# Twelve decoder stages on one Trainium2 core: other numbers of identity products at 18 calls and in the attention ramps, query rows issued from ScalarE, LayerNorm tails of two feed-forwards reordered

## The reference, cut to what matters

```
x = LN(x + L0_attn(x));   x = LN(x + L0_xattn(ctx, x)); x = LN(x + L0_ffn(x))
x = LN(x + L1_attn(x));   x = LN(x + L1_xattn(x, ctx)); x = LN(x + L1_ffn(x))
x = LN(x + L2_attn(x));   x = LN(x + L2_xattn(x, ctx)); x = LN(x + L2_ffn(x))
x = LN(x + L3_attn(x));   x = LN(x + L3_xattn(ctx, x)); x = LN(x + L3_ffn(x))
```

## Time and profile before

| | |
|---|---|
| median of 3 runs | 2351.48 us (2344.88 to 2352.47) |
| the profiled execution | 2345.65 us |
| its span, first to last instruction | 2343.8 us |
| TensorE busy (share of the span) | 2112.0 us (90%), 25065 products |
| VectorE, ScalarE, GpSimd busy | 1330.4, 1129.5, 967.9 us |
| identity products of `stay_busy`, L583 | 575 |

### The profile page before, as it was taken

How to read it: one execution, slowest core, us unless ns; L and a number is a source line. 1 busy time by engine, 2 the same in 40 slices (tenths; PEclk the granted TensorE clock), 3 DMA queues, 4 the chain that set the end, 5 groups by cost and what they waited for, 6 DMA issues and landing times. The chain is left out here.

```text
span 2343.8 us, 60484 instructions
## 1 busy us (share of the span) xinstructions
PE 2112.0 (90%) x25065; PEld 1276.9 (54%) x25109; DVE 1330.4 (57%) x3369; ACT 1129.5 (48%) x2592; POOL 967.9 (41%) x865
## 2 busy tenths in 40 slices
PE   5998999889987899999999999999879989899894
PEld 3445666645543555555555555555544557455563
DVE  3535454447835776777777776767436533467233
ACT  1333455115532676766667776767514402235321
POOL 2010000020125887878888787878310023200023
PEclk9999999999998999999999999999989989989897
DMA  2110000000002021211121111211000024000321
GB/s 68 26 36 1 2 1 1 1 15 6 3 1 75 18 61 28 48 41 43 36 52 33 49 33 37 60 27 43 18 8 13 2 61 143 16 13 2 103 69 44
DMA packets 70577, 78.54 MB, mean 34 GB/s; under 512 B 10624, under 2 KB 48649, under 8 KB 70306
## 3 DMA queue, kind: packets, MB, share of 16 engines
q1 hardware_dynamic: 64114, 61.75, 10.1%
q0 software_dynamic: 3696, 10.56, 1.5%
q10 hardware_dynamic: 2496, 2.36, 0.5%
HBM read 40.90 MB, written 6.82 MB: 20 GB/s over the span
## 5 line engine op out<-in xcount | busy, mean ns | idle before, releaser
L3573 POOL TENSOR_TENSOR l1fb_rinv<-l1fb_ssq,neghalf 128x8 f32<-128x8 f32 x192 | 316.0, 1646 | 160.6 <-DVE l1fb_ssq L3616 158.1
L3716 ACT ACTIVATE l1fb_p<-ps,l1fb_shift 128x64 f32<-128x64 f32 x768 | 177.7, 315 | 159.0 <-PE ps L3873 137.7
L3575 POOL TENSOR_TENSOR l1fb_qk<-l1fb_qk,l1fb_r 128x512 f32<-128x512 f32 x192 | 244.1, 1271 | 0.0
L3780 PE MATMUL ps<-l1fb_wqkv,l1fb_xs 128*128 128x512 f32 x384 | 219.2, 654 | 6.3 <-DVE l1fb_r L3626 6.2
L3577 POOL TENSOR_TENSOR l1fb_qk<-l1fb_qk,l1fb_rinv 128x512 f32<-128x512 f32 x192 | 200.2, 1042 | 15.1
L3626 DVE TENSOR_TENSOR l1fb_r<-ps,l1fb_turn_tab 128x256 f32<-128x256 f32 x384 | 142.8, 413 | 0.0
L3623 DVE TENSOR_TENSOR l1fb_qk<-ps,l1fb_turn_tab 128x512 f32<-128x512 f32 x192 | 132.2, 689 | 14.4 <-POOL l1fb_qk L3575 12.5
L583 PE MATMUL ps<-ident_b 128*128 128x512 bf16 x575 | 133.8, 389 | 3.5 <-PEq L671 1.7
L3614 DVE TENSOR_REDUCE l1fb_ssq<-l1fb_sq 128x8 f32<-128x512 f32 x192 | 129.7, 675 | 2.7 <-ACT l1fb_sq L3696 2.7
L3696 ACT ACTIVATE l1fb_sq<-ps 128x512 f32<-128x512 f32 x192 | 118.7, 618 | 11.7 <-PE ps L3780 10.9
L3724 ACT ACTIVATE l1fb_both<-ps 128x512 f32<-128x512 f32 (+1 forms) x194 | 117.3, 604 | 8.3 <-PE ps L3873 7.8
(11 more groups left out here) (728 smaller groups left out, 4817.9 us busy)
## 6 DMA issues: line engine op xcount, KB each, us to landing
l1fb_v<-l1fb_v SPq DMA_DIRECT2D x48, 260.0 KB, 4.3
l1fb_v<-l1fb_v SPq DMA_DIRECT2D x48, 195.0 KB, 3.9
l1fb_wqkv<-in_L_ffn_Wqkv SPq DMA_DIRECT2D x24, 256.0 KB, 2.9
l3f_w<-in_L_ffn_W SPq DMA_DIRECT2D x21, 256.0 KB, 6.8
l1fb_wqkv<-in_L_ffn_Wqkv SPq DMA_DIRECT2D x6, 512.0 KB, 5.1
l1fb_wo<-in_L_ffn_Wo SPq DMA_DIRECT2D x6, 512.0 KB, 4.1
l1fb_w<-in_L_ffn_W SPq DMA_DIRECT2D x6, 341.0 KB, 3.0
l3f_xs<-zeros SPq DMA_DIRECT2D x1, 1344.0 KB, 7.1
```

The source lines that it names most:

```text
L3573: nc.gpsimd.tensor_tensor(w.rinv[:, u, :], w.ssq[:, u, :], chip.neghalf[:, 0:8], ALU.pow).then_inc(*w.unit_norm.end(f"rinv{u}"))
L3575: nc.gpsimd.tensor_tensor(w.qk[:, u, :], w.qk[:, u, :], fp(w.r2), ALU.add).then_inc(*w.unit_norm.end(f"add{u}"))
L3716: last = nc.scalar.activation(w.p[:, c % 2, q, j, :], ps[:, SCORE_BANK + j, q * SEEN:(q + 1) * SEEN], ACT.Exp, bias=w.shift[:, c, j, q:q + 1])
L3780: nc.tensor.matmul(ps[:, PROJ_BANK(u), :], w.xs[:, x.odd, q * P:(q + 1) * P], w.wqkv[:, col:col + 512], start=True, stop=True)\
```

## The change

Numbers of identity products (`stay_busy`) at 18 calls, before -> after:

| stage | head | end |
|---|---|---|
| l0_attn | 18 -> 26, 24 -> 18 | |
| l0_xattn | 19 -> 23 | 24 -> 28 |
| l0_ffn | | 6 -> 8 |
| l1_attn | 9 -> 13, 37 -> 31 | 7 -> 11 |
| l1_xattn | | 12 -> 16 |
| l1_ffn (enter, leave) | 14 -> 20 | 44 -> 27 |
| l2_attn | 24 -> 18 | 9 -> 14 |
| l2_xattn | | 6 -> 10 |
| l2_ffn | 95 -> 99 | 80 -> 78 |
| l3_attn | | 13 -> 18 |
| l3_xattn | 28 -> 24 | |

In the ramp of the three stages without a mask, each step gets two more in front of the first bank's product. `ahead` becomes a table by slot: l2_attn 8 in front of group 0 as before and now 8 in front of group 2, l1_attn now 5 in front of group 0. The four query DMAs of batch 0 go from SyncE to ScalarE, right behind ScalarE's copy of the queries (in l1_attn behind its copy of `xT1`, since VectorE makes the queries there). The tail of L1_ffn is done for all four batches together with four sets of buffers, and that of L2_ffn batch by batch with each batch's last step put behind the next batch's statistics.

```diff
+def strips_load_begin(eng, h, q1, q_ready):
+    eng.wait_ge(*h.padded_q.of(0))
+    eng.wait_ge(*q_ready)
+    strips_load_queries(eng, h, 0, 0, q1)
...
 def strips_load(eng, h, i, q1, k1, q_ready, k_ready):
...
-        for at in range(0, P, STRIP):
-            eng.dma_start(h.q[at:at + h.hd, :, b, :], q1[at:at + STRIP, i, n * S:(n + 1) * S]).then_inc(*h.heads_in[b].landed())
+        if b:
+            strips_load_queries(eng, h, i, n, q1)
...
-        if (t, u, i, p) == (0, 0, 0, 0):
-            stay_busy(nc, chip, 3 + h.bank(b, g, u, i), ahead)
+        if (u, i, p) == (0, 0, 0) and t in ahead:
+            if n_of(b, g, u, i) >= 3:
+                eng.wait_ge(*h.exped.of(n_of(b, g, u, i) - 3))
+            stay_busy(nc, chip, 3 + h.bank(b, g, u, i), ahead[t])
...
                     scores_free(slot, u, i)
+                    stay_busy(nc, chip, h.bank(*h.group(slot), u, i), 2 - 2 * i)
...
             nc.scalar.activation(q1[:, 0, :], ps[:, 7, :], ACT.Copy, scale=scale).then_inc(*act.end("q0"))
+            strips_load_begin(eng, h, q1, act.done("q0"))
...
@@ l2_ffn @@
-                tails_dve(nc, eng, chip, t[PAIR * pair:], dve, pool, pair, lambda i: gathered[PAIR * pair + i].of(QT - 1),
+            for b in range(B):
+                eng.wait_ge(*gathered[b].of(QT - 1))
+                nc.vector.tensor_tensor(fp(t[b].y), of(back, b), of(kept, b), ALU.add).then_inc(*dve.end(f"sum{b}"))
+                tail_stats(nc, eng, t[b], dve, b)
+                tail_var(nc, eng, chip, t[b], dve, b)
+                if b:
+                    tail_normed(nc, eng, chip, t[b - 1], dve, pool, b - 1)
+            tail_normed(nc, eng, chip, t[B - 1], dve, pool, B - 1)
...
@@ l1_ffn_leave @@
-                nc.vector.tensor_copy(fp(xb), chip.x_tok[:, b, :, :]).then_inc(*dve.end("x"))
-                tail_dve(nc, eng, chip, t, dve, pool, b, chip.ps[:, b, 0:S].rearrange("p (t d) -> p t d", t=QT), fp(xb))
+                eng.wait_ge(*pe.done(f"y{b}"))
+                nc.vector.tensor_tensor(fp(t[b].y), chip.ps[:, b, 0:S].rearrange("p (t d) -> p t d", t=QT), chip.x_tok[:, b, :, :], ALU.add)\
+                    .then_inc(*dve.end(f"sum{b}"))
+            for b in range(B):
+                tail_stats(nc, eng, t[b], dve, b)
+            for b in range(B):
+                tail_var(nc, eng, chip, t[b], dve, b)
+            for b in range(B):
+                tail_normed(nc, eng, chip, t[b], dve, pool, b)
```

More of the change, by code:

```diff
@@ L123, in tail_pool, with tail_stats, tail_var, tail_normed @@
     nc.gpsimd.tensor_tensor(fp(t.rstd), fp(t.rstd), chip.neghalf[:, 0:QT], ALU.pow).then_inc(*pool.end("rstd" + of))
+def tail_stats(nc, eng, t, dve, b):
+    eng.wait_ge(*dve.done(f"sum{b}"))
+    for q in range(QT):
+        last = nc.vector.bn_stats(t.stats[:, q, :], t.y[:, q, :])
+    last.then_inc(*dve.end(f"stats{b}"))
+def tail_var(nc, eng, chip, t, dve, b):
+    eng.wait_ge(*dve.done(f"stats{b}"))
+    nc.vector.memset(chip.scratch[:, 4 + b:5 + b], 0.0)
+    for q in range(QT):
+        last = nc.vector.bn_aggr(t.mv[:, q, :], t.stats[:, q, :])
+    last.then_inc(*dve.end(f"var{b}"))
+def tail_normed(nc, eng, chip, t, dve, pool, b):
+    eng.wait_ge(*pool.done(f"rstd{b}"))
+    for q in range(QT):
+        last = nc.vector.tensor_scalar(chip.x_tok[:, b, q, :], t.y[:, q, :], t.mv[:, q, 0:1], t.rstd[:, q:q + 1], ALU.subtract, ALU.mult)
+    last.then_inc(*dve.end(f"normed{b}"))
+def tail_root(nc, eng, chip, t, dve, pool, b):
+    eng.wait_ge(*dve.done(f"var{b}"))
+    nc.gpsimd.tensor_tensor(fp(t.rstd), t.mv[:, :, 1], chip.eps[:, 0:QT], ALU.add).then_inc(*pool.end(f"vareps{b}"))
+    eng.wait_ge(*pool.done(f"vareps{b}"))
+    nc.gpsimd.tensor_tensor(fp(t.rstd), fp(t.rstd), chip.neghalf[:, 0:QT], ALU.pow).then_inc(*pool.end(f"rstd{b}"))
 def named(names, i):
@@ L316, in strips_pad_keys, with strips_pe @@
     last.then_inc(*h.padded_k.one())
-def strips_pe(nc, eng, chip, h, vhead, v_ready, mask=None, early=None, late=None, ahead=0):
+def strips_pe(nc, eng, chip, h, vhead, v_ready, mask=None, early=None, late=None, ahead={}):
     ps = chip.ps
+    n_of = lambda b, g, u, i: 2 * h.pair(b, g, u) + i
     def scores_free(t, u, i):
@@ L1086, in early @@
                     eng.wait_ge(*dve.done("v1"))
[L1088 to L1089 removed]
+            strips_pe(nc, eng, chip, h, lambda i: i, lambda i: dve.done(f"v{i}"), early=early, ahead={0: 8, 2: 8})
+            stay_busy(nc, chip, 0, 14)
 LAMBDA_INIT = 0.8 - 0.6 * float(np.exp(-0.3 * 12))
@@ L1266, in late @@
                     strips_out(nc, eng, chip, h, b, attT, w["L1_attn_Wo"], None)
-            strips_pe(nc, eng, chip, h, lambda i: i // 2, lambda i: dve.done(f"v{i}"), early=early, late=late)
-            stay_busy(nc, chip, 0, 7)
+            strips_pe(nc, eng, chip, h, lambda i: i // 2, lambda i: dve.done(f"v{i}"), early=early, late=late, ahead={0: 5})
+            stay_busy(nc, chip, 0, 11)
 def paired(names):
@@ L2733, in _ @@
                     .then_inc(*gathered[q // QT].landed())
-            for pair in range(B // PAIR):
-                tails_pool(nc, eng, chip, t[PAIR * pair:], dve, pool, pair)
+            for b in range(B):
+                tail_root(nc, eng, chip, t[b], dve, pool, b)
         @block.vector
@@ L3348, in l1_ffn_leave @@
     with ExitStack() as ctx:
-        sb = lambda n, s, dt=F32: ctx.enter_context(nc.sbuf_tensor(f"l1fl_{n}", s, dt))
         pe_s, dve_s, act_s, pool_s, loads = stage_sems(nc, ctx, "l1fl")
-        t = Tail(nc, ctx, "l1fl")
-        xb = sb("xb", [P, QT, D])
-        pe, dve, pool = Steps(pe_s, ["y"]), Steps(dve_s, ["x"] + TAIL_DVE), Steps(pool_s, TAIL_POOL)
+        t = [Tail(nc, ctx, f"l1fl{b}") for b in range(B)]
+        each = lambda name: [f"{name}{b}" for b in range(B)]
+        pe, dve = Steps(pe_s, each("y")), Steps(dve_s, each("sum") + each("stats") + each("var") + each("normed"))
+        pool = Steps(pool_s, [f"{name}{b}" for b in range(B) for name in TAIL_POOL])
         block = ctx.enter_context(nc.Block())
@@ L3373, in _ @@
                     last = nc.tensor.transpose(chip.ps[:, b, q * P:(q + 1) * P], f.xr[:, b, q * P:(q + 1) * P], chip.ident[:, :])
-                last.then_inc(*pe.end("y"))
-            stay_busy(nc, chip, 5, 44)
+                last.then_inc(*pe.end(f"y{b}"))
+            stay_busy(nc, chip, 5, 27)
 class FfnWork:
```

49 lines of the change are left out of this document (27 added, 22 removed).

## The result

The changed kernel takes 2334.98 us (median of 6 runs, 2326.19 to 2340.53) where the kernel before takes 2351.97 beside it. The ratio is 0.9937, 95% interval [0.9918, 0.9956]. Run twice more on other chips it gave 0.9907 [0.987, 0.9945] and 0.9946 [0.9924, 0.9968]. So it is faster by about 15 us by the ratio (17 by the two medians), where 30.5 against the median had been forecast: the direction was right, the size about half.

What follows compares the result with a forecast made beforehand. TensorE was taken as the bound in nine low-clock stretches, besides its waits for DMAs and barriers. Terms -9.8 + 6.1 + 0 - 4.0 - 0.3 - 18.5 = -26.5 us from 2345.65 gave 2319.2, adjusted to 2321 us; range 2309 to 2340.

Steps and rivals of the forecast that it cites:

- part 1: Four strips stages: batch 0's query DMAs on ScalarE make key DMAs land sooner, -9.8 us (5.7 to 11.4).
- part 5: Nine low-clock stretches: filled waits hold TensorE's clock, three quarters of 25 us regained, -18.5 us (0 to -25).
- Rival (b): l1_attn and l3_xattn: transfers bound the landing, nothing moves there, 4.1 us less gain, 2325 us; chance 0.14.
- The side condition: Strips stages' heads: identity products cut by 4 or 6, 0.9 or 1.3 us, so they end before the new landing.
- Part 2: Ramps of l1_attn, l2_attn, l3_xattn: two more products per step and the `ahead` products cost +6.1 us (3 to 16).
- The forecast of steps: l3_xattn's ramp: all sixteen steps 2.24 us or, behind an `early`, 0.44 longer than before, at clock 1.00.
- Rival (c): Ramps: added products do not hold the high clock and run at the low one, +9.9 us, 2356; chance 0.05.
- Part 3: Heads and ends: twelve calls grow by 2 to 8 products, each covered by a longer wait, cost 0.
- Part 4: Tails: L1_ffn's batches together -4.0 us (-3.5 to -4.4), L2_ffn's last block -0.3 us (0 to -1.3).
- the nine stretches: Low-clock stretches just behind added work, 61.3 us together at 1.2 GHz, TensorE busy 58.7; few should stay at 0.50.
- (a): Whole kernel: the clock does not follow, stretches fall elsewhere, only parts 1, 2 and 4 remain, 2338 us; chance 0.19.
- some 40 us: Whole kernel: the clock's low time must fall by this much, or the prediction is wrong.

Runs made afterwards that it cites:

- The four parts alone: Kernel before with one part each: batch 0's queries on ScalarE, 0.9987; ramps' products, 0.9972; two tails, 0.9977; longer series at heads and ends, 0.9957.
- `e_tails`: Kernel before with the two tails alone (L1_ffn's batches together with 27 products, L2_ffn's batch by batch with 78): ratio 0.9977.
- `a_hl`: Changed kernel with longer identity series at the four heads (25, 36, 22, 49) and products in L1_ffn's layers: 2319.94 us, ratio 0.9875.
- `e_start`: Kernel before with only batch 0's query DMAs moved to ScalarE and four heads cut by 4 or 6 products: ratio 0.9987.

## Why the prediction was right or wrong

**Direction and the two largest terms' signs: right.** The sum of -26.5 us was -8.0 without the clock and -18.5 of clock. Measured are -3.6 +- 0.8 without the clock, and 25 and 41 us less low clock on the two chips, 33 in the mean, which at 0.337 is -11. The four parts alone sum to -1.0 +- 2.1 at equal clock, as they should within the errors, but to 61 us less low clock: that is where they do not add. Two terms are too large, part 1 and part 5, each by some 7 us.

**Part 1, -9.8 us: wrong, the step that failed first.** The keys did leave 2.7 to 3.1 us sooner. What failed is the step from there to the landing. For l0_attn and l2_attn the text took the full 2.85 us ("the issue sets the pace") and the profiles gave 1.5 and 2.2. For l1_attn and l3_xattn it took 1.8 and 2.3 and they gave -1.1 and +0.3. Together that is 2.9 us for 9.8, and alone the part measured -2.3 +- 0.7 in the executions. The reading behind it was of the DMA share: 0.27 and 0.49 looked like room, and "the first transfers had idle engines". In the changed kernel the share stands at such a value from the first packet to the last, in l1_attn already before the change (0.20, 0.28, 0.27, 0.27 in windows of 2 us from 495 to 503). Rival (b), that the transfers bound these two stages, was right and had been given 0.14. It had no term for the loss in l1_attn, where packets take longer on two queues. The rule of the Trainium skill (Trainium Kernel Development and Optimization, Key Constraints), that issuing from several engines saves issue time only, agrees with gains that stay below the 2.85 us of issue time, 1.5, 2.2 and 0.3; it doesn't tell of l1_attn's loss of 1.1 us. The side condition was missed too: the heads' products were cut for a landing that did not come, and left waits of 5.0 and 3.2 us.

**Part 2, +6.1 us: right in kind, a little high**: +4.5 +- 0.8, within its ends of 3 and 16. The forecast of steps held at 2.24 us. Rival (c), ramps at the low clock, did not appear.

**Part 3, 0: right**: -1.5 +- 0.8 at equal clock.

**Part 4, -4.3 us**: the tail is 4.4 us shorter and L1_ffn's end 4.1 us (4.3 in `e_tails`), where -4.0 was taken: right, with the mechanism that the text named, products at the low clock that end at 1737.28 (forecast 1736.7) behind a tail that starts 0.5 us later and ends at 1736.33 (forecast 1735.8). In the text's sum, "4 x 1.1 less 0.5" is 3.9 and not the 3.4 that it adds; 3.5 was measured, so the slip lies in the words. At equal clock the part measured -1.7 +- 0.7 in the whole. Where the other 2.6 us would be was not found. L2_ffn's last block is one batch as forecast, and its stage no shorter (83.7 us in both profiles).

**Part 5, -18.5 us: right mechanism, wrong size.** Two factors were off. The price: "a full stretch gives back 45% of its busy time" came to 25 us for 61.3 us, 0.41, and three quarters of it; the executions give 0.337, and l3_xattn, with the longest stretch, some 0.25 by its stage. The amount: three quarters of 61.3 us are 46, and in total 33 went. At the nine places themselves the forecast held: by the clock records of the changed kernel's trace six of the nine stretches are gone, 47.7 us, among them those of both ramps, and three with 13.6 us stay (at the start of the slots in l1_attn and l3_xattn, and in l2_ffn). What failed is the assumption that nothing comes in their place: the trace as a whole has only 10.5 us less, so some 37 us are at places that had none before or had less. In this pair of profiles l0_attn went from 3.4 to 13.5, l3_attn from 3.4 to 10.2 and L1_ffn's layers, which the change leaves alone, from 31.8 to 42.3. These places vary like that from one execution to the next: another profile of the same changed program has 31.9 in the layers. So a pair of profiles does not tell where low clock went, and only the sums over executions count. By them part of (a) was in the result as well, and it was not "the clock does not follow" but "it follows where the wait is filled": `a_hl`, which filled the waits that part 1 left open and those in the layers, has 62 us less low clock than the changed kernel. Of the signs that the text named, the nine stretches (six of them gone), the ramp steps and L1_ffn's tail were seen; "some 40 us" of low time was met on one chip of two; the two full landings of 2.8 us were not. On the size of the clock's share, the Trainium skill (TensorE: Matmul & The Clock Gate, What's actually happening) puts the penalty of the ramp to full clock at under 1% of a typical kernel's span, and the prediction took that for all low stretches together. This kernel has 24 of them, and the runs go beyond it: the kernel without the products is 2.0% above the one before, and `a_hl` 1.25% below it.

The range held the result only because it reached to 2340 for rival (a); the sum itself was not met. A sum whose largest term depends on where the clock falls is better priced from the scatter of executions than from the busy share of the stretches alone.

## What to carry to other kernels

Plot the times of a kernel's executions against their granted clock: the slope estimates the price of a low clock in this kernel, near the low clock that the executions have, and the distance at equal clock is what an edit does apart from it. Fill the waits of TensorE that the profile shows after a change, not those of before; a DMA that is issued sooner has to be seen landing sooner before the products ahead of it are cut. Count a landing from the work that both kernels wait for, not from an issue that the edit itself has moved. A DMA share that stands flat over a whole load is a limit, however low it is. Moving half of a batch's transfers to a second queue is worth trying stage by stage: here it gave 2.2 us in one and took 1.1 in another.

## What was not expected of the hardware

At l0_attn's head VectorE converts the mask while GpSimd copies one row beside it. In 17 profiles this took one of three lengths, 2.50 us (two), 4.99 (six) or 6.94 (nine), and the same program had both of the longer ones. VectorE and GpSimd in the changed kernel:

```profile
26.35 6.94 DVE L792 TENSOR_SCALAR l0a_mf<-w_L_attn_mask 128x512 f32<-128x512 int32 x1 [0.33 <-PEq L691]
```
```profile
26.60 6.95 POOL L305 COPY l0a_rows<-w_L_attn_b_kvu 1x128 f32<-1x128 f32 x1
```

and VectorE in the kernel with the first part alone (`e_start`):

```profile
26.20 2.50 DVE L754 TENSOR_SCALAR l0a_mf<-w_L_attn_mask 128x512 f32<-128x512 int32 x1 [0.32 <-PEq L653]
```

The copy of one row starts 0.25 us later and ends 0.25 us later each time: it lasts as long as VectorE's. By the Trainium skill (SBUF — State Buffer, SBUF: two separate sides) the two share a port pair as an exclusive lock that one of them holds for its whole instruction; the equal ends agree with that, and the three lengths are not explained by it. It shifts this stage by up to 4.4 us from one profile to the next, which is one more reason to compare stages over several.

The other was l1_attn's landing: 9.0 us after the keys' copy for eight DMAs on one queue, 10.7 us for the same eight on two, with 0.084 us for a packet and then 0.114 to 0.129.
